# Attention and a mixture of experts on one core: three written lists of steps in a new order

## What is computed

```python
x = x + layernorm(attn(layernorm(x)))
x = x + layernorm(ffn(layernorm(x)))

# attn: 32 heads of width 8
q, k, v = split(x @ Wqkv.T + b)
a = einsum('bthd,bshd->bhts', q, k)
ctx = einsum('bhts,bshd->bthd', a, v)
ctx = groupnorm(ctx) * gn_w + gn_b        # over time, within a head
return ctx @ out_w.T + out_b

# ffn: _ffn(x, g, u, d) = (silu(x @ g.T) * (x @ u.T)) @ d.T, hidden width 704
shared = _ffn(xf, shared_gate, shared_up, shared_down)
topw, topi = top_k(softmax(xf @ gate_w.T), 2)
routed = sum over the experts e of _ffn(xf, gw[e], uw[e], dw[e]) * comb[:, e]
return shared + routed
```

## Time and profile before

| | |
|---|---|
| Median of 3 runs | 1039.66 us |
| The profiled execution's own time | 1039.01 us |
| Its span | 1037.0 us |
| TensorE busy | 829.5 us (80%) |
| VectorE busy | 660.7 us (64%) |
| ScalarE busy | 479.8 us (46%) |
| GpSimd busy | 305.1 us (29%) |
| Mean granted TensorE clock | 0.908 of full speed |
| Batches 1 to 6 | 71.7 to 388.0 us |
| Last batch | 388.0 to 438.5 us |
| Tail, up to the last inversion | 438.5 to 506.9 us |
| Routed tiles begin | 517.4 us |

### The profile page before, as it was taken

The page is one execution under the profiler, slowest core; times in us unless marked ns, Lnnn a source line. Parts: engine busy times, 40 slices in busy tenths (PEclk is TensorE's granted clock), DMA queues, the critical chain, the costliest instruction groups (busy, mean ns, idle before and its releaser), DMA issues.

```text
span 1037.0 us, 22586 instructions
## 1 busy us (share of the span) xinstructions
PE 829.5 (80%) x6598; PEld 680.2 (66%) x6599; DVE 660.7 (64%) x1708; ACT 479.8 (46%) x1065; POOL 305.1 (29%) x342
## 2 busy tenths in 40 slices
PE   4477979787979797747499999999999999999100
PEld 2355666666666665535288988988898888888100
DVE  4677878787878887879545555555555554555165
ACT  2042536263635364523155555555555555555233
POOL 1010000000000000007724455455445544554224
PEclk9888999898989898877799999999999999999655
DMA  4122222323232313130113222223322332233673
GB/s 167 41 90 79 85 104 78 111 72 117 72 117 72 118 52 117 52 102 11 31 23 52 41 46 51 47 41 51 50 43 46 52 46 41 46 47 43 178 220 108
DMA packets 56254, 76.69 MB, mean 74 GB/s; under 512 B 8256, under 2 KB 51008, under 8 KB 55040
## 3 DMA queue, kind: packets, MB, share of 16 engines
q1 hardware_dynamic: 41232, 55.33, 15.7%
q0 software_dynamic: 14976, 20.78, 12.6%
HBM read 48.96 MB, written 27.26 MB: 74 GB/s over the span
## 4 chain that ended last, share of the span: by engine, by line
PE 52%; DVE 18%; DMA 13%; issue 7%; ACT 5%; POOL 3%; ACTq 0%; POOLq 0%; DVEq 0%; SPq 0%
PE ps L779 27%; PE ps L794 14%; DMA acc_d<-ysb,idxc 10%; PE ps L876 3%; DVE mx L1077 3%; PE ps L840 3%; POOL attw L515 2%; DMA x_d<-att 2%; DVE wgu L1110 1%; DVE small L1439 1%; PE ps L927 1%; DVE hf L1051 1%; DVE att L1203 1%; ACT wdn L755 1%; ACT ysb L624 1%
## 5 line engine op out<-in xcount | busy, mean ns | idle before, releaser
L779 PE MATMUL ps<-att,wgu 128*128 128x256 f16 x2574 | 320.7, 274 | 1.9 <-DVE att L1371 1.6
L1051 DVE SCALAR_TENSOR_TENSOR hf<-ps,sc,silu 128x256 f32<-128x256 f32 x330 | 159.4, 483 | 226.3 <-ACT silu L594 203.1
L794 PE MATMUL ps<-wdn,hT 128*128 (+1 forms) x1870 | 266.8, 282 | 13.6 <-DVE hT L1061 13.5
L779 PEld LDWEIGHTS ps<-att,wgu 128*128 x2574 | 251.5, 98 | 34.4 <-issue 4.8
L594 ACT ACTIVATE silu<-ps,sc 128x256 f32<-128x256 f32 x275 | 130.1, 474 | 262.9 <-PE ps L779 262.9
L794 PEld LDWEIGHTS ps<-wdn,hT 128*128 128x128 f16 x1870 | 187.0, 101 | 47.8 <-DVE hT L1061 18.7
L779 PE MATMUL ps<-xhl,wgu 128*128 128x256 f16 x1056 | 144.0, 293 | 10.6 <-DVE hf L1051 7.9
L488 POOL TENSOR_TENSOR rstd<-ve,mhalf 128x4 f32<-128x4 f32 (+1 forms) x32 | 29.8, 930 | 387.5 <-DVE ve L1036 335.9
L545 POOL DMA_INDIRECT acc_d<-ysb,idxc x78 | 125.1, 1604 | 58.0 <-POOL idxc L541 31.1
L779 PEld LDWEIGHTS ps<-xhl,wgu 128*128 128x128 f16 x1056 | 109.7, 106 | 39.7 <-DVE hf L1051 9.9
L608 ACT CAST hT<-hf 128x256 f16<-128x256 f32 x275 | 109.7, 399 | 27.3 <-DVE hf L1051 26.1
(11 more groups left out here) (185 smaller groups left out, 941.8 us busy)
## 6 DMA issues: line engine op xcount, KB each, us to landing
wgu<-in_gu SPq DMA_DIRECT2D x8, 1408.0 KB, 6.1
att<-in_x SPq DMA_DIRECT2D x16, 512.0 KB, 4.1
wdn<-in_dn SPq DMA_DIRECT2D x8, 768.0 KB, 7.9
x_d<-att SPq DMA_DIRECT2D x8, 512.0 KB, 2.9
xn_d<-att SPq DMA_DIRECT2D x8, 512.0 KB, 3.0
acc_d<-ysb SPq DMA_DIRECT2D x16, 256.0 KB, 3.3
wgu<-x_d SPq DMA_DIRECT2D x8, 512.0 KB, 4.5
wdn<-acc_d SPq DMA_DIRECT2D x8, 512.0 KB, 6.0
```

The costliest lines, as they stand in the source:

```text
L779: ins = te.matmul(o, slot_gu(slot, hw, k, j), x(hx, k), start=(n == 0), stop=(n == len(TERMS) - 1))
L794: ins = te.matmul(y_bank(u, tt), h(hh), slot_dn(slot, c, hw), start=(c == 0 and n == 0), stop=(c == FC - 1 and n == 1))
L1051: v.scalar_tensor_tensor(out=hf[lo:P, c % 2 * TW:(c % 2 + 1) * TW], in0=up, scalar=scale_of(slot, 1, lo, P), in1=silu[lo:P, c % 2 * TW:(c ...
```

## The change

The same steps stand in the three lists in a new order. No step is added or taken away, and no other line differs. The new `ORDER` has one line of text more, so every line number behind it is larger by one in the changed kernel (L1051 becomes L1052). The start and the parts of the lists that the text speaks of:

```diff
-ORDER = [("G", 0), ("ln1_stats",), ("H", 0), ("ctx",), ("G", 1), ("ctx_out",), ("channel_stats",), ("H", 1), ("G", 2), ("group_mean",), ("H", 2),
...
-         ("H", 5), ("D", 3), ("prep_max", 0), ("out_out",), ("turn1",), ("turn1_out",), ("prep_max", 1), ("prep_max", 2), ("prep_diag",), ("prep_spread",), ("G", 6), ("D", 4),
-         ("H", 6), ("lno_stats",), ("q",), ("q_out",), ("G", 7), ("D", 5), ("H", 7), ("lno_apply",), ("kv", 0), ("prep_scale",),
...
+ORDER = [("ln1_stats",), ("ctx",), ("ctx_out",), ("G", 0), ("channel_stats",), ("G", 1), ("H", 0), ("group_mean",), ("G", 2), ("H", 1),
...
+         ("H", 4), ("out",), ("G", 6), ("H", 5), ("prep_max", 0), ("prep_max", 1), ("prep_max", 2), ("out_out",), ("H", 6), ("turn1",),
+         ("turn1_out",), ("lno_stats",), ("prep_diag",), ("G", 7), ("H", 7), ("q",), ("q_out",), ("prep_spread",), ("lno_apply",),
...
+         ("prep", 1), ("D", 6), ("prep", 2), ("turn2",), ("prep", 3), ("H", 10), ("turn2_out",), ("H", 11), ("state",), ("D", 7),
+         ("state_out",), ("G", 11), ("D", 8), ("xhl",), ("D", 9), ("D", 10), ("logits",), ("logits_out",), ("D", 11)]
...
+LAST_ORDER = [("route_probs", 0), ("ctx",), ("ctx_out",), ("G", 0), ("G", 1), ("channel_stats",), ("H", 0), ("group_mean",), ("group_var",),
+         ("H", 1), ("ctx_norm",), ("H", 2), ("H", 3), ("G", 2), ("G", 3), ("D", 0), ("out",), ("prep_max", 0), ("out_out",),
+         ("prep_max", 1), ("prep_max", 2), ("lno_stats",), ("prep_diag",), ("H", 4), ("G", 4), ("lno_apply",), ("route_top1", 0),
...
+TAIL = [("route_top1", 1), ("G", 0), ("G", 1), ("route_top2", 1), ("H", 0), ("route_slots",), ("H", 1), ("route_positions",), ("H", 2),
+         ("D", 0), ("one_hots", 0), ("G", 2), ("G", 3), ("invert", 0), ("G", 4), ("prep_max", 0), ("one_hots", 1), ("H", 3), ("H", 4),
```

More of the change, by code:

```diff
@@ L37 @@
 NSLOT = E + 1
-ORDER = [("G", 0), ("ln1_stats",), ("H", 0), ("ctx",), ("G", 1), ("ctx_out",), ("channel_stats",), ("H", 1), ("G", 2), ("group_mean",), ("H", 2),
[5 rows of a table removed]
-         ("turn2",), ("turn2_out",), ("prep", 2), ("H", 11), ("state",), ("state_out",), ("xhl",), ("logits",), ("D", 9), ("prep", 3),
-         ("logits_out",), ("D", 10), ("D", 11)]
-FIRST_HALF = ("ln1_stats", "ln1_apply", "turn1", "turn1_out", "q", "q_out", "kv", "kv_out", "state", "state_out")
-LAST_ORDER = [("G", 0), ("ctx",), ("H", 0), ("route_probs", 0), ("ctx_out",), ("G", 1), ("channel_stats",), ("H", 1), ("G", 2), ("group_mean",),
-              ("H", 2), ("G", 3), ("group_var",), ("G", 4), ("H", 3), ("ctx_norm",), ("D", 0), ("D", 1), ("out",), ("out_out",), ("D", 2), ("G", 5),
-              ("H", 4), ("lno_stats",), ("prep_max", 0), ("prep_max", 1), ("H", 5), ("lno_apply",), ("G", 6), ("prep_max", 2), ("prep_diag",), ("prep_spread",), ("D", 3),
[4 rows of a table removed]
@@ L58 @@
[L58 to L64, removed]
+ORDER = [("ln1_stats",), ("ctx",), ("ctx_out",), ("G", 0), ("channel_stats",), ("G", 1), ("H", 0), ("group_mean",), ("G", 2), ("H", 1),
+         ("group_var",), ("G", 3), ("G", 4), ("H", 2), ("G", 5), ("ctx_norm",), ("D", 0), ("D", 1), ("H", 3), ("D", 2), ("ln1_apply",),
+         ("H", 4), ("out",), ("G", 6), ("H", 5), ("prep_max", 0), ("prep_max", 1), ("prep_max", 2), ("out_out",), ("H", 6), ("turn1",),
+         ("turn1_out",), ("lno_stats",), ("prep_diag",), ("G", 7), ("H", 7), ("q",), ("q_out",), ("prep_spread",), ("lno_apply",),
[4 rows of a table added]
@@ new lines @@
+TAIL = [("route_top1", 1), ("G", 0), ("G", 1), ("route_top2", 1), ("H", 0), ("route_slots",), ("H", 1), ("route_positions",), ("H", 2),
[3 rows of a table added]
+         ("prep_spread",), ("G", 8), ("G", 9), ("one_hots", 4), ("invert", 4), ("G", 10), ("prep_scale",), ("H", 8), ("one_hots", 5),
+         ("invert", 5), ("D", 6), ("prep", 0), ("H", 9), ("prep", 1), ("H", 10), ("G", 11), ("prep", 2), ("one_hots", 6), ("D", 7),
+         ("D", 8), ("prep", 3), ("H", 11), ("invert", 6), ("D", 9), ("one_hots", 7), ("D", 10), ("D", 11), ("invert", 7),
+         ("route_indices",)]
```

## The result

| | before | changed |
|---|---|---|
| Median | 1039.99 us (4 runs, 1039.30 to 1041.45) | 987.25 us (4 runs, 983.00 to 1000.62) |
| Profiled execution (its span) | 1039.0 us (1037.0) | 988.1 us (986.4) |
| TensorE busy | 829.5 us | 817.9 us |
| VectorE busy | 660.7 us | 657.5 us |
| GpSimd busy | 305.1 us | 307.0 us |

The ratio of the times is 0.9478, with a 95% interval of 0.9444 to 0.9511: the changed kernel is faster by 5.2%. (The run of 1000.62 us was a disturbed one, at a clock of 0.883; it is in the table's median and is left out of the ratio.) The forecast was 989 us.

A forecast was written before the change was run, and what follows sets the result against it. Batches were held bound by the order in which two nearly full engines, VectorE and TensorE, hand over work. Savings of 1.0 (batch 0), 40.3 (six bodies), 4.7 (last batch) and 4.3 (tail), 50.3 us, gave 989 us; range 975 to 1012.

The forecast's parts named there:

- The forecast case: Whole kernel: handover waits go and the time falls to 989 us; chance 0.55.
- What bounds a body: Batches 1 to 6: handover waits between VectorE and TensorE; 52.7 us a body, VectorE busy 42.4, 45.3 without a clock fall.
- The step on `prep_spread`: Middle of a body: spread placed behind G 6, turn1, G 7 and q; TensorE's 5.5 us pause and VectorE's 3.64 go.
- The step on `G 7` ahead of `q`: Middle of a body: G 7 no longer queued behind q on TensorE, so VectorE's second silu wait of 3.70 us goes.
- The clock after the logits: Around the logits: the clock falls again, slowing D 11 and G 0; 0.7 us added per body (0 to 1.7).
- the rival by which the clock does not fall at all: After the logits: the clock holds, bodies stay at 45.3 us, whole time 985 us; chance 0.24.
- Batch 0: First batch: q goes some 2.3 us earlier, two prep pieces move ahead of xhl; gain 1.0 us (0 to 2.3).
- Last batch and tail: After the six bodies: shorter VectorE waits; gains of 4.7 us (2 to 6) and 4.3 us (1 to 7).
- no longer end it: Tail: POOL's 48 one-hots take 34 us but start some 12 us earlier, so they do not end the tail.
- TensorE as the bound: Bodies: short pauses and half clock on TensorE give 49.6 us a body, 1013 us in all; chance 0.15.
- The staged weights: Start of bodies: weights landing over 19 us after issue hold up the maxima; some 1041 us at 20 us; chance 0.03.

## Why the prediction was right

The forecast case held, and the main mechanism with it. Point by point:

**What bounds a body**: right. VectorE's 42.4 us stayed (42.05 to 42.19) and only waits went. Of the forecast 45.3 us without a fall of the clock, 42.4 + 0.9 + 2.0, the four bodies without a fall took 44.9 to 45.8 (45.15 on the mean), with the 0.9 us at `ctx_out` measured at 0.9. TensorE's 41.2 us of work was 41.6 to 41.7 us at a clock of 1.00, and the "about 1 us of TensorE's idle time at each of the two", `turn1` and `q`, is 0.9 and 0.9.

**The step on `prep_spread`**: right, and larger than it was booked. It had 3.64 us of a body, some 22 us of six. Moved by itself it gave 43.8 us, and put back in part, together with `prep_diag`, it took about 22.

**The step on `G 7` ahead of `q`** ("The 3.70 us go"): the wait went, but for a cause other than the one given. "At the second, `G 7` was queued behind `q`" holds for TensorE's queue and decides nothing: with `G 7` alone ahead of `q` the wait was 3.74 us, and with `G 7` left behind `q` but the spread moved it was gone. What decides is how late `q` itself is, by the spread, and that ScalarE's copies of `q_out` and chunk 5 stand in its queue ahead of H 7's silu. The prediction walked VectorE's and TensorE's queues through this place, and not ScalarE's. As both moves are in the change, the sum did not suffer.

**The clock after the logits**: "I let it fall again", 0.7 us on the mean body. It fell in two bodies of six, at 1.7 and 1.9 us, 0.6 on the mean. The size is right, partly by luck, and the picture is not: 0 or 1.8, not 0.7 each time. The prediction had read the fall in body 3 alone, and in the trace of the kernel before both kinds already stood side by side: behind the logits, each time after a pause of 0.74 to 0.75 us, it fell in three of the five bodies after the first and not in the other two. The half-clock stretch in the middle of the body is gone, as the 1.00 of whole bodies shows. Of the rival by which the clock does not fall at all, four bodies are like it and two are not. The rule on long idle gaps in the Trainium skill ("TensorE: Matmul & The Clock Gate", section "Why this matters for your kernels") agrees with the stretch that went with the pause of 5.5 us. The rule leaves open why the level at `ctx` differs between bodies in which the engines do the same, and the runs leave it open too.

**Batch 0**: too small, 1.0 us for 3.8, above even the upper bound of 2.3. The step had only `q` go earlier. TensorE's 5.54 us before the spread went altogether, and on VectorE, whose waits in this batch were no part of the working, the waits at `kv_out` (1.9 us) and `out_out` (1.6 us) are gone. The spread's move does not account for it: moved by itself it left batch 0 at 42.3 us, so most of the gain is from other moves in the list.

**Last batch and tail**: too large, 9.0 us for 6.0. The last batch's 3.5 us wait in one piece is 3.1, as forecast. But the prediction had "about 0.3" left of the waits before `out_out`, the first prep and the `hf` other than H 0, and 1.9 us of them are there (1.4 of the 1.6 at `hf`, and 0.5). The 1.4 us stand behind `G 2` and `G 3` at the half clock told of above, for which the prediction had 0.5 us:

```profile
DVE st L1225 <- ACT att L668: 3.1, 1, 3.1
DVE hf L1052 <- ACT silu L595: 1.6, 2, 1.4
DVE att L1254 <- PE ps L877: 0.5, 1, 0.5
```

In the tail the waits at `hf` fell from 3.7 to 1.7 us, where 0.7 was forecast, and the last inversion's did not fall: 1.8 us, was 1.6, forecast 0.3.

```profile
DVE attw L1359 <- PE ps L915: 1.8, 1, 1.8
DVE hf L1052 <- ACT silu L598: 0.9, 1, 0.9
DVE hf L1052 <- ACT silu L595: 0.8, 1, 0.8
```

The sentence that failed here is that the one-hots "no longer end it"; their ending the tail was one of the prediction's own signs of being wrong. They do start some 12 us earlier in the tail, and then wait for inversions; the last six end at 455.99, and the indices are made from 456.40 on:

```profile
412.70 11.16 POOL L516 TENSOR_SCALAR attw<-iota,attw 128x128 f16<-128x128 f16 x18 [36.80 <-DVEq L1343]
...
438.55 12.39 POOL L516 TENSOR_SCALAR attw<-iota,attw 128x128 f16<-128x128 f16 x12 [3.53 <-PE ps L915]
452.40 3.59 POOL L516 TENSOR_SCALAR attw<-iota,attw 128x128 f16<-128x128 f16 x6 [1.46 <-PE ps L915]
```

Four waits of 8.7 us in all stand between them, where there was one of 1.50 us before. This came with the clock. In the execution of the same kernel in which the clock held, GpSimd's waits were 4.4 us in all, the last inversion's wait was 0.3 us, as forecast, and the tail took 62.1 us, a gain of 6.0, more than the forecast's 4.3:

```profile
DVE attw L1359 <- PE ps L915: 0.3, 1, 0.3
```

So the missing 1.7 us of the tail come with a fall of the clock, for which the prediction's tail had no term; without it the forecast was too small.

**The rivals**: TensorE as the bound fell (its idle time in a body is 3.3 us against VectorE's 2.8, and VectorE's waits are few). The staged weights cost nothing: in body 3 the loads landed 6.9 and 9.7 us after their issue, and VectorE shows no wait at the maxima. (The threshold of that rival, "over 19 us after its issue", does not follow from its own terms: 7.9 + 9 + 6.7 is 23.6 us.)

## What to carry to other kernels

Where two engines are each over 80% full, look for the first late handover of a stage and move that step behind work which is ready; the waits behind it can be its echo, as both were here, and go with it. A wait's row names the engine that was late, not why: walk the queue of **that** engine (here ScalarE's) before moving what fed it. Read the clock in all repeats of a stage, and not in one: here it fell in three of six. And where a stage's length differs between executions of one kernel (62.1 or 65.4 us here), measure that first, since a gain of 2 us in it can't be read from one profile.

## What the runs showed of the hardware

**GpSimd slows beside one VectorE operation.** A one-hot of 128x128 takes 0.60 us on GpSimd (median 607 ns of 48 in the changed kernel, longest 2341; before 597, longest 1789). A slow one, and VectorE in its time:

```profile
440.34 2.22 POOL L516 TENSOR_SCALAR attw<-iota,attw 128x128 f16<-128x128 f16 x1
```

```profile
440.50 1.67 DVE L1111 SCALAR_TENSOR_TENSOR wgu<-att,pw,wgu 128x1408 f16<-128x1408 f32 x1
```

It took 1.61 us more than the median, about as long as VectorE's operation (1.67 us), so it seems to stand still until that ends. The Trainium skill ("SBUF — State Buffer", section "Who interferes with whom") says that GpSimd and VectorE share a pair of ports, which an operation of VectorE with two inputs in SBUF holds for its whole length against a GpSimd operation that reads SBUF, and that the one that starts first gets it. L1111 is such an operation. The length agrees; the order the trace does not show, since the profile has the one-hot start 0.16 us before it. The 48 one-hots took 32.4 us in all before and 34.6 in the changed kernel. The prediction's 34 us was scaled up from 36 of them, some of which stood beside a `prep` already.

**One kernel, three chips.** The kernel before took 1040.6 us on one chip and 1071.7 and 1073.3 us on two others. For the new lists the profiled executions show where: the bodies are the same (44.9 to 46.9 us on each), and what follows the last inversion takes 530.0 us in the first one and 559.3 and 560.1 us in the others. The changed kernel's ratio held: 0.9478, 0.9477 and 0.9481. In that part the `G` matmuls take the same time (321.7, 320.7 and 321.8 us), and TensorE's idle time just before them is 1.9 us on the first chip and 28.0 and 27.2 on the others, nearly all of it waits for VectorE's `hf`. What makes that late was not looked into.
